# Keys projected from hi and lo parts in three products, with both parts of x copied by DMA to buffers of their own

## What is computed

```python
qkv = x @ w_qkv.T
q, k, v = jnp.split(qkv, 3, axis=-1)            # then split into heads
L = jnp.einsum('bhqd,bhkd->bhqk', q, k) * scale
k_y = _split_heads(x @ w_ky.T)
L_y = jnp.einsum('bhqd,bhkd->bhqk', q, k_y) * scale
agg = jnp.sum(jnp.exp(jnp.clip(L_y, -15.0, 15.0)) * mask, axis=-1, keepdims=True) + EPS
r = _eml(L, agg)                                # log(|L| + eps) - log(agg + eps)
w = jax.nn.softplus(r) * mask
A = w / (jnp.sum(w, axis=-1, keepdims=True) + EPS)
out = jnp.einsum('bhqk,bhkd->bhqd', A, v)       # then @ w_proj.T
```

## Time and profile before

| | us |
|---|---|
| median of 3 runs (1239.84 to 1242.23) | 1241.31 |
| the profiled execution | 1241.82 |
| its span on the core | 1240.10 |

### The profile page before, as it was taken

How to read it: one execution, slowest core, us unless ns; L and a number is a source line. 1 busy time by engine, 2 the same in 40 slices (tenths; PEclk the granted TensorE clock), 3 DMA queues, 4 the chain that set the end, 5 groups by cost and what they waited for, 6 DMA issues and landing times.

```text
span 1240.1 us, 23985 instructions
## 1 busy us (share of the span) xinstructions
PE 1182.6 (95%) x8222; PEld 804.6 (65%) x8222; DVE 715.4 (58%) x1178; ACT 658.9 (53%) x1004; POOL 206.2 (17%) x238
## 2 busy tenths in 40 slices
PE   5899999999999999879999999999999999999997
PEld 2444454444444444437888888888888888888886
DVE  3567779787878787775444435344344353443444
ACT  4688989898888888756124233232242332322411
POOL 2433333433333333210000000000000000000000
PEclk7999999999999999999999999999999999999999
DMA  4455767576776756178000100000000000000010
GB/s 150 107 142 135 219 152 230 155 229 173 204 202 177 213 157 149 44 221 298 34 34 1 34 18 17 34 0 34 17 0 34 17 17 34 0 34 17 0 34 18
DMA packets 62544, 117.28 MB, mean 95 GB/s; under 512 B 8992, under 2 KB 14624, under 8 KB 62496
## 3 DMA queue, kind: packets, MB, share of 16 engines
q1 hardware_dynamic: 62064, 116.12, 32.9%
q10 hardware_dynamic: 432, 0.52, 0.2%
HBM read 46.35 MB, written 19.92 MB: 53 GB/s over the span
## 4 chain that ended last, share of the span: by engine, by line
PE 78%; DVE 9%; issue 5%; ACT 5%; DMA 1%; POOL 1%; DVEq 0%; ACTq 0%; POOLq 0%; SPq 0%
PE score_banks L1312 53%; PE acc_bank L1224 8%; PE score_banks L1196 6%; DVE w_ring L867 4%; PE misc_bank L1151 3%; PE misc_bank L1292 2%; PE misc_bank L1188 2%; ACT w_ring L633 2%; ACT e_ring L626 1%; DVE e_ring L858 1%; PE misc_bank L1255 1%; DVE base_v L920 1%; DVE e_ring L852 1%; PE misc_bank L1159 1%; PE misc_bank L1271 1%
## 5 line engine op out<-in xcount | busy, mean ns | idle before, releaser
L705 ACT ACTIVATE f_h_full<-score_banks,f_scales 128x512 f32<-128x512 f32 x128 | 87.5, 689 | 340.8 <-PE score_banks L1312 340.7
L867 DVE TENSOR_TENSOR w_ring<-score_banks,keep 128x1024 int32<-128x1024 int32 (+1 forms) x192 | 194.1, 1040 | 26.6 <-PE score_banks L1196 25.8
L1312 PE MATMUL score_banks<-f_ha_hi,f_w_all 128*128 128x512 f32 x512 | 204.0, 399 | 0.0
L1312 PE MATMUL score_banks<-f_hb_hi,f_w_all 128*128 128x512 f32 x512 | 203.6, 398 | 0.0
L1312 PE MATMUL score_banks<-f_hb_lo,f_w_all 128*128 128x512 f32 x512 | 201.6, 394 | 0.0
L1312 PE MATMUL score_banks<-f_ha_lo,f_w_all 128*128 128x512 f32 x512 | 200.8, 392 | 0.0
L633 ACT ACTIVATE w_ring<-w_ring 128x1024 f32<-128x1024 f32 (+1 forms) x192 | 172.5, 918 | 24.4 <-DVE w_ring L867 24.3
L626 ACT ACTIVATE e_ring<-score_banks 128x1024 f32<-128x1024 f32 (+1 forms) x192 | 158.4, 877 | 39.2 <-PE score_banks L1196 38.1
L501 POOL TENSOR_SCALAR_AFFINE_SELECT e_ring<-e_ring 128x512 f32<-128x512 f32 (+1 forms) x96 | 79.1, 824 | 288.2 <-DVE e_ring L858 144.8
L1045 DVE CAST f_ha_hi<-f_h_full 128x512 fp32r<-128x512 f32 x64 | 27.3, 427 | 160.4 <-ACT f_h_full L705 160.4
L1312 PEld LDWEIGHTS score_banks<-f_ha_hi,f_w_all 128*128 128x128 f32 x512 | 96.1, 188 | 24.6
(11 more groups left out here) (143 smaller groups left out, 1758.0 us busy)
## 6 DMA issues: line engine op xcount, KB each, us to landing
piece<-in_wf SPq DMA_DIRECT2D x44, 256.0 KB, 2.9
wf_copy<-piece SPq DMA_DIRECT2D x44, 256.0 KB, 2.9
ky_stack<-ky_hi SPq DMA_DIRECT2D x64, 128.0 KB, 2.4
ky_stack<-ky_lo SPq DMA_DIRECT2D x64, 128.0 KB, 2.4
k_stack<-k_hi SPq DMA_DIRECT2D x64, 128.0 KB, 2.7
k_stack<-k_lo SPq DMA_DIRECT2D x64, 128.0 KB, 2.6
f_w_all<-wf_copy SPq DMA_DIRECT2D x2, 4096.0 KB, 25.8
f_x_turn<-x SPq DMA_DIRECT2D x9, 512.0 KB, 3.3
```

The costliest lines, as they stand in the source:

```text
L705: nc.scalar.activation(h_full[m % 2][:], f_bank[m % F_RING], ACT.Gelu, scale=scales[:, 1 + layer, m:m + 1]).then_inc(gelu_done, 1)
L867: nc.vector.tensor_tensor(w_ring[:, t % RING, 2 * i:2 * i + 2, 0:cols].bitcast(I32), pair_banks(place(t, i), cols).bitcast(I32), keep[:, a ...
L1312: mm = nc.tensor.matmul(out, left.bitcast(dt), right.bitcast(dt), start=first and n == 0, stop=last and n == 1)
```

## The change

The projection of keys becomes three F32R products for each of its two steps, six matmuls for a unit where two stood. For this the weights of the keys are split too (`split_weights(2)` on ACT and DVE at the start, after the other work there), and PE waits for that at the start in place of the unsplit weights. Since `xq_hi` and `xq_lo` hold another batch in the second half, SP copies both, 512 KB each, to buffers of their own, `xk_hi` and `xk_lo`, once per batch in the first half. Three waits go with this: SP's copy waits until the keys of the batch before are projected and x is split; ACT's next split of x waits for the copy; PE's projection waits for the copy instead of xv. The zone of buffers that end with the ky scores grows from 80 to 92 KB.

```diff
-        w_hi, w_lo = of_y("w_hi", [P, DT, 2, D], F32R), of_y("w_lo", [P, DT, 2, D], F32R)
+        xk_hi, xk_lo = of_y("xk_hi", [P, DT, T], F32R), of_y("xk_lo", [P, DT, T], F32R)
+        w_hi, w_lo = of_y("w_hi", [P, DT, 3, D], F32R), of_y("w_lo", [P, DT, 3, D], F32R)
...
+            def copy_x(b):
+                reach_alone(sp, k_ready, 2 * b, sp_passed)
+                reach_alone(sp, xq_split, b + 1, sp_passed)
+                for there, here in ((xk_hi, xq_hi), (xk_lo, xq_lo)):
+                    sp.dma_start(there[:].bitcast(F32), here[:].bitcast(F32)).then_inc(xk_in, 16)
...
                 if 3 in w:
                     stack_k(k.shift(-1), 0)
+                if k.half == 0:
+                    copy_x(k.batch)
                 if check:
                     load_piece(k, 0, check)
...
             def split_x(b):
                 reach(act, xq_in, 16 * (b + 1))
                 reach(act, q_ready, 2 * b)
+                reach(act, xk_in, 32 * b)
...
+            split_weights(2)
             run(slot, ending, act.Fori)
...
             make_keep()
+            split_weights(2, 3)
             run(slot, ending, dve.Fori)
...
-            def project_t(u, kind, x, done):
-                m = slice(P * u.half, P * u.half + P)
-                for kt in range(DT):
-                    mm = nc.tensor.matmul(misc[:], w_in[:, kt, kind, m], x[:, kt, :], start=kt == 0, stop=kt == DT - 1)
-                mm.then_inc(done, 1)
-
-            def project_split(u, kind, done, kts=range(DT), bank=misc):
+            def project_split(u, kind, done, kts=range(DT), bank=misc, x_hi=xq_hi, x_lo=xq_lo):
...
             def k_proj(u):
                 take_misc((k_made, u.index + 1))
-                reach(pe, xv_in, 16 * (u.batch + 1))
-                project_t(u, 2, xv, k_ready)
+                reach(pe, xk_in, 32 * (u.batch + 1))
+                project_split(u, 2, k_ready, x_hi=xk_hi, x_lo=xk_lo)
...
-            pe.wait_ge(kind_made[2], 2 * DT)
+            pe.wait_ge(w_lo_made, 3)
```

More of the change, by code:

```diff
@@ L95, in program @@
         at = nc.sbuf_base + -nc.sbuf_base % 32
-        END_ZONE, Y_ZONE, SHARED = 23 * 1024, 80 * 1024, 185 * 1024 - 128
+        END_ZONE, Y_ZONE, SHARED = 23 * 1024, 92 * 1024, 185 * 1024 - 128
         def place(zone, start, size):
@@ L205, in program @@
         xq_hi_made, xq_split = sem("xq_hi_made"), sem("xq_split")
-        xq_in, xv_in, xn_in = sem("xq_in"), sem("xv_in"), sem("xn_in")
+        xq_in, xv_in, xn_in, xk_in = sem("xq_in"), sem("xv_in"), sem("xn_in"), sem("xk_in")
         q_ready, ky_ready, k_ready, v_ready = sem("q_ready"), sem("ky_ready"), sem("k_ready"), sem("v_ready")
@@ L1158, in project_split @@
                     hi, lo = w_hi[:, kt, kind, m], w_lo[:, kt, kind, m]
-                    nc.tensor.matmul(bank[:], hi, xq_hi[:, kt, :], start=kt == 0, stop=False)
-                    nc.tensor.matmul(bank[:], lo, xq_hi[:, kt, :], start=False, stop=False)
-                    mm = nc.tensor.matmul(bank[:], hi, xq_lo[:, kt, :], start=False, stop=kt == DT - 1)
+                    nc.tensor.matmul(bank[:], hi, x_hi[:, kt, :], start=kt == 0, stop=False)
+                    nc.tensor.matmul(bank[:], lo, x_hi[:, kt, :], start=False, stop=False)
+                    mm = nc.tensor.matmul(bank[:], hi, x_lo[:, kt, :], start=False, stop=kt == DT - 1)
                 if DT - 1 in kts:
```

## The result

| | median us (executions) | ratio to the kernel before, 95% interval |
|---|---|---|
| kernel before | 1241.32 (1239.69 to 1242.23) | |
| changed kernel | 1248.35 (1246.32 to 1255.15) | 1.0056 [1.0041, 1.0072] |

The change makes the kernel slower by 7.0 us; the forecast was 3.0 slower. The profiled execution of the changed kernel is the longest of its six: 1255.15 us, with a span of 1253.4. The other five lie between 1246.3 and 1248.5.

The account below looks back on a forecast made before the run. The prediction took PE as busiest, with ACT's logs a second path right under it: 1241.8 - 2.0 for the matmuls + 5.0 for the copies' stops = 1244.8 us; forecast 1242 to 1247, wide range 1238.5 to 1250.5.

Parts of the forecast that it names:

- The gain of the matmuls: Key projection on PE: 6.6 us freed over 16 units, 2.0 us gained because PE then waits for ACT's logs.
- Rival 2: PE is the bound, copies hidden, all 6.6 us of the key projection return: 1234.7 us, chance 0.09.
- ACT's own unbroken row of work: In the loop, ACT's logs hang on its gapless work, not on the key projection; 0.21 us a pass can be won.
- The start: At the kernel's start, the third weight cast and subtraction finish before PE's first scores: no cost, cover 1.4 us.
- the added waits: The new waits of SP, ACT and PE around the copies cost nothing; PE's is covered by some 13 us.
- the feed-forward part: The change touches only the attention part; the feed-forward part stays unchanged.
- The copies: On SP's queue in loop first halves, two 512 KB copies make what is queued behind, including qc_lo, 1.8 us later.
- the scores named: PE's first scores that read qc_lo, at the fourth beat of each loop pass's first half: PE stops about 1.0 us.
- the room of 0.9: Between qc_lo's landing at 281.65 and PE's first scores that read it at 282.54: 0.9 us.
- The price of the stops: PE's stop for qc_lo is paid in full: 1.0 us in each of five loop passes, 5.0 us.
- rival 3: The first piece lands late, ACT stops too, each loop pass loses 2.0 us or more: 1249.3 us, chance 0.17.

Follow-up runs that it names:

- products alone: The changed kernel without the copies, its six key matmuls reading the split x itself (the next batch's in second halves): 1240.96 us, 0.9988 of the kernel before.
- the four kernels that make the products without the loss: The changed kernel without copies; with copies at the second half's end; with first qc stacks ahead of the second piece; with both: 0.9988, 0.9989, 0.9998, 0.9997.
- moved cast: The changed kernel with copies at the second half's end and ACT's cast of q_hi moved from beat 3 to beat 4 in first halves: 1246.24 us, 1.0033.
- tiny copies: The kernel before with three, four or five 2 KB issues on SP between the qc_hi and qc_lo stacks, loop first halves: 1250.16, 1264.06, 1264.76 us.
- copies alone: The changed kernel with both copies kept but unread, and keys projected as before by two float32 matmuls: 1251.55 us, 1.0079 of the kernel before.
- three tiny issues: The kernel before with three 2 KB issues on SP between the stacks of qc_hi and qc_lo in the loop's first halves: 1250.16 us, 1.0068.
- filled stop: The kernel before with four 2 KB issues, and PE making the query projection's first half three times ahead of the scores reading qc_lo: 1252.49 us, 1.0093.
- four tiny issues: The kernel before with four 2 KB issues on SP between the stacks of qc_hi and qc_lo in the loop's first halves: 1264.06 us, 1.0153.

## Why the prediction came out as it did

**What bounds the kernel: right. The gain of the matmuls: not contradicted.** PE waits for the logs behind the six matmuls in both halves, 0.17 and 0.25 us, close to the forecast (0.2 to 0.4). Of 0.41 freed, 0.10 came back in the first half; the products alone measured 0.9988, the forecast's 2.0 us is 0.9984, and the interval leaves room for both that and nothing. The forecast had half of it, 1.05 us, come from the loop; there the trace of the products alone shows no gain over the five passes. Rival 2, all 6.6 us, is refuted by the four kernels that make the products without the loss: 0.9947 lies below all their intervals. The Trainium skill, page "Perfetto Trace Analysis", section "Identifying the Most-Contended Engine", would have the busiest engine improved first, with a warning that PE's busy time is a poor measure; here 6.6 us were taken off PE and at most 3 came back, so the runs do not bear that rule out at this place. One step was incomplete: the forecast said that ACT's logs hang on ACT's own unbroken row of work. The moved cast shows that this row hangs in its turn on PE's query projection.

**The start, the added waits, the feed-forward part: right.** The first scores start at 18.45 us (18.64 in the earlier trace rows), PE never waits for the copies, and the feed-forward part is unchanged. The ending, in which the forecast had no loss, is 2.2 us longer in the profiled execution, by the clock.

**The copies: the mechanism right, the time on which qc_lo lands nearly so.** SP's issue of the second piece moved with the landing of wf_copy, qc_lo stood behind it, and PE stopped at exactly the scores named. The two issues held SP for 0.48 and 0.60 us, not the 0.35 each that was taken. qc_lo came 2.2 us late in the third pass, 1.8 forecast; the room of 0.9 was right, as the tiny copies show too (1.84 us of issues, 0.92 us of stop). The rate taken from the earlier trace rows was nearer than the fabric's rate that the Trainium skill gives (page "DMA: Bandwidth & Descriptors", section "Where 436 GB/s comes from"): by that the stop would have been 0.5 us, and it was 1.15 to 2.56. In the first pass, with the longest stop, qc_lo took 4.7 us from issue to landing, in the other four 3.2 to 3.5. What slowed it there is not shown by any run, nor why in the other four it lands 0.4 to 0.6 us later behind the start of the pass than in the copies alone, so that the stops are 1.6 us on the mean over all five and not 0.9.

**The price of the stops: the term that was mis-sized.** "It is paid in full: so 1.0 us in each of five passes, 5.0 us" is right for a stop behind which the clock stays: such passes grow by what PE stands still. The term is too small for two reasons. The stops of the changed kernel were 1.15 to 2.56 us long in the profiled execution, 8.1 in all. And the sum had the granted clock at nothing: the forecast looked at it only in stretches where it was 1.00, and had no term for what a stop does to it; two falls cost 4.7 us in that loop. Where the stops did have the forecast's size, in the copies alone and with three tiny issues, the kernels are 10.2 and 8.6 us over the kernel before by their medians, and in the profiled loops 6.1 and 9.3 us were lost for 4.5 and 4.6 us of stops. The passes without a fall are 66.4 to 67.3 us long, 66.6 to 66.9 forecast; those with one are 69.6 and 71.4. By the ratios the copies are at +9.8 and the products at -1.5, together +8.3; measured is +7.0.

**Luck in the range.** The measured 1248.35 us lies over the 1242 to 1247 of the forecast itself and within the wide range of 1238.5 to 1250.5, whose upper part was there for rival 3. That the range holds it is luck: rival 3, 1249.3, gives nearly the measured time for another reason: ACT did not stop for its pieces there as that rival said (0.2 us in the whole span), and of the five stops only the first was 2.0 us or more.

The Trainium skill, page "TensorE: Matmul & The Clock Gate", section "What's actually happening", says that a gate lets all or half of the pulses through, by how busy PE has been of late. The levels here are those two, 1.00 and 0.50 of the full clock, and the filled stop agrees that it is PE's own activity that counts.

## What to carry to other kernels

A copy that no engine waits for can still be dear by what is queued behind it: look for the next landing that its queue waits for, then for the issue behind that, and for the room of the engine that reads it; moving either the copy or the urgent issue is a cure. A short stop of a nearly saturated PE costs its length, and two to three times its length where the clock of the microseconds behind it falls, so a stop's price is read from the granted clock too, not only from the bracket in the timeline. And microseconds freed on the busiest engine are worth only as much as the second path, which has to be followed back beyond the first engine on it.

## What was not expected of the hardware

Stops of PE of 0.9 to 1.7 us, in a stretch where it is otherwise busy nine tenths of the time, were followed by a fall of the granted clock to half in some passes and not in others: in the changed kernel behind a stop of 1.35 us and not behind 1.38 or 1.70; with four tiny issues behind each of five stops of 1.52 to 1.56; with three tiny issues behind stops of 0.89, 0.91 and 0.87 us and not behind 1.02 and 0.89. With stops of 2.2 us it fell every time (all of these in one profiled execution of each kernel). A pass with the mean of its ten microseconds at 0.66 is 2.6 us longer than one without a fall in the changed kernel; at 0.83, 1.5 us in the copies alone (68.24 against a mean of 66.7 of the neighbours). Repeated matmuls whose result is thrown away by the next, put into the stop, kept the clock at 1.00 in the loop. And the clock falls without a late qc_lo too: the last 32 to 36 us of the attention's ending had a mean of 0.95 in the kernel before, and from 0.80 to 1.00 in the others, with copies and without.
